# First stage of a graph network kernel: four counted superblocks ahead of the gathered ones, the other eleven between them, and the stage's buffers laid out anew

## The reference

```python
# gated layer
src_h = h[src] @ W_msg.T + b_msg
msg = src_h + edge_embed[clip(edge_type, 0, 8)]
messages = segment_sum(msg, dst, num_segments=N)
x = layernorm(x + gru_cell(messages, x))
# three layers, edges turned round, with a self loop on every node
h = concat(x[dst], edge_attr @ enc)      # the first one adds them
agg = segment_sum(h, src)
x' = relu(batchnorm(agg @ w1 + b1)) @ w2 + b2
# result: layernorm(x + layers(x))
```

## Time and profile before

| | us |
|---|---|
| median of three runs | 5869.93 |
| profiled execution | 5869.73 |
| its span | 5868.0 |
| PE busy | 5116.0 (87%) |
| DVE busy | 3763.8 (64%) |
| ACT busy | 3325.4 (57%) |
| POOL busy | 4223.4 (72%) |

### The profile page before, as it was taken

The page is one execution under the profiler, slowest core; times in us unless marked ns, Lnnn a source line. Parts: engine busy times, 40 slices in busy tenths (PEclk is TensorE's granted clock), DMA queues, the critical chain, the costliest instruction groups (busy, mean ns, idle before and its releaser), DMA issues.

```text
span 5868.0 us, 88444 instructions
## 1 busy us (share of the span) xinstructions
PE 5116.0 (87%) x26429; PEld 3281.9 (56%) x26429; DVE 3763.8 (64%) x14165; ACT 3325.4 (57%) x4432; POOL 4223.4 (72%) x4243
## 2 busy tenths in 40 slices
PE   4498888888888387777779999998999998999998
PEld 1144444444444144444447777776777776777776
DVE  8699999999999376666744444443444443444444
ACT  1177777777777222222347677665666665666665
POOL 6777777777777777777157777776777776777775
PEclk9999999999999677877679999999999999999999
DMA  8287778788878444444256666667767777666765
GB/s 282 62 182 188 176 180 185 182 191 200 186 180 194 98 117 123 118 122 121 68 193 201 198 212 210 211 212 219 207 200 213 213 212 235 205 196 206 206 204 163
DMA packets 1068180, 1066.43 MB, mean 182 GB/s; under 512 B 494051, under 2 KB 784501, under 8 KB 1067701
## 3 DMA queue, kind: packets, MB, share of 16 engines
q1 hardware_dynamic: 889573, 782.05, 47.6%
q0 software_dynamic: 178128, 278.65, 17.9%
HBM read 747.21 MB, written 216.68 MB: 164 GB/s over the span
## 4 chain that ended last, share of the span: by engine, by line
PE 44%; POOL 10%; issue 4%; DMA 3%; DVE 2%; ACT 1%; SPq 1%; DVEq 0%; ACTq 0%
PE ps L2965 27%; POOL GL L3051 7%; PE ps L2935 5%; POOL BIG L3033 3%; PE ps L2848 2%; PE ps L2809 2%; PE ps L2899 2%; PE ps L2810 2%; DVE BIG L2197 1%; PE ps L2909 1%; PE ps L2910 1%; DMA MS<-counts 1%; PE ps L2811 1%; DMA h_dense<-PCL 1%; PE ps L2914 0%
## 5 line engine op out<-in xcount | busy, mean ns | idle before, releaser
L3051 POOL DMA_INDIRECT GL<-h_gathered,IDXA x2058 | 2122.4, 1031 | 899.7 <-issue 615.4
L2965 PE MATMUL ps<-MSR,HP 128*128 128x512 f32 (+1 forms) x9000 | 2292.0, 402 | 56.0 <-ACT MSR L2575 36.6
L2575 ACT CAST MSR<-MS 128x1024 fp32r<-128x1024 uint8 (+1 forms) x1500 | 1509.3, 1029 | 959.0 <-PE ps L2965 867.5
L2965 PEld LDWEIGHTS ps<-MSR,HP 128*128 128x128 f32 x9000 | 1644.5, 190 | 449.4 <-ACT MSR L2575 57.9
L3017 POOL DMA_INDIRECT rec_q<-BIG x1563 | 1514.0, 969 | 521.6 <-issue 443.4
L2258 DVE CAST MSR<-MS 128x1024 fp32r<-128x1024 uint8 (+1 forms) x750 | 524.5, 700 | 1049.0 <-PE ps L2965 951.4
L2750 PE MATMUL ps<-MTB,XPS 128*128 128x512 bf16 x4410 | 1195.2, 387 | 1.0 <-DMA XPS<-x_parts 0.8
L2461 ACT CAST MTB<-MT 128x1024 bf16<-128x1024 uint8 x735 | 768.1, 1045 | 57.9 <-PE ps L2750 14.5
L3033 POOL DMA_INDIRECT BIG<-x_parts,SRCq x611 | 582.2, 953 | 188.1 <-issue 180.7
L2457 ACT CAST MT<-ps 128x512 uint16<-128x512 f32 x735 | 427.4, 582 | 343.6 <-PE ps L2733 328.9
L2750 PEld LDWEIGHTS ps<-MTB,XPS 128*128 128x128 bf16 x4410 | 414.7, 98 | 216.3 <-issue 20.0
(11 more groups left out here) (248 smaller groups left out, 5970.8 us busy)
## 6 DMA issues: line engine op xcount, KB each, us to landing
MS<-counts SPq DMA_DIRECT2D x1080, 256.0 KB, 3.4
counts<-BIG SPq DMA_DIRECT2D x360, 256.0 KB
XPS<-x_parts SPq DMA_DIRECT2D x192, 384.0 KB
GL<-h_gathered,IDXA POOLq DMA_INDIRECT x2058
rec_q<-BIG POOLq DMA_INDIRECT x1563
rec_q<-BIG SPq DMA_DIRECT2D x44, 490.0 KB, 10.9
HTI<-h_cols SPq DMA_DIRECT2D x72, 256.0 KB
h_dense<-PCL SPq DMA_DIRECT2D x30, 512.0 KB, 8.0
```

Of the source, the lines that this page charges most:

```text
L2575: s.copy(MSR[:, g % RM, :, 0:w].rearrange("p t (c s) -> p t c s", s=P), MSB[:, i % MR, 0:4 * w].rearrange("p (c h s t) -> p h t c s", h=2, ...
L2965: got = t.matmul(bank[:, 0:w], HP[:, d, part, :], MSR[:, g % RM, d % 2, 0:w], start=d + part == 0, stop=lay > 0 and d + part == BD, skip_g ...
L3051: g.indirect_dma_start(out=GL[:, r % LR, i, 0:3 * P], out_offset=None, in_=HGd[lay], in_offset=bass.IndirectOffsetOnAxis(ap=IDXA[:, a + i: ...
```

## The change

`node_groups()` now gives 0, 1, 2, 3, 15, 4, 16, 5, 17, 6, 18, 7, 19, 8, 9, 20, 10, 21, 11, 22, 12, 23, 13, 14, 24. DVE and SP wait at the stage's start for the counts stored and the records made (SP also for the last tiles placed); the wait for the scatters stands at slot PRELUDE = 66, the first gathered one (on DVE at that slot's one-hots). SP's index loads start there, and their chunks are spread over the slots behind it. POOL's own wait for the scatters stays; its gathers lose the wait that kept them near PE for the first 16 groups. `XG` and `SX` move behind the other buffers in BIG2. There are 409 slots in place of 408.

```diff
 def node_groups():
-    by_counts, gathered = list(range(JX)), list(range(JX, SG))
-    got = [by_counts.pop(0)]
-    while by_counts or gathered:
-        got += by_counts[:1] + gathered[:1]
-        by_counts, gathered = by_counts[1:], gathered[1:]
+    got, by_counts = list(range(4)), list(range(4, JX))
+    gathered = list(range(JX, SG))
+    for k, u in enumerate(gathered):
+        got.append(u)
+        n = len(gathered) - 1
+        got += by_counts[len(by_counts) * k // n:len(by_counts) * (k + 1) // n]
     return got
...
-INDEX_AT = [range(NS // IX * k // len(SLOTS), NS // IX * (k + 1) // len(SLOTS)) for k in range(len(SLOTS))]
+PRELUDE = GATHERED[QS0]
+
+def index_at(k):
+    if k < PRELUDE:
+        return range(0)
+    a, n = k - PRELUDE, len(SLOTS) - PRELUDE
+    return range(NS // IX * a // n, NS // IX * (a + 1) // n)
...
 def summed_beside(r):
-    return max(2 * r - 2, GATHERED[QS0 + r - QR] + 1 if r >= QR else 0)
+    return GATHERED[QS0 + r - QR] + 1 if r >= QR else 0
...
         ring = carve(BIG2)
-        XG = ring(QR * GT * XW // 2)...
-        SX = ring(QR * GT * 128)...
         SXD = ring(DR * GT * 128)...
...
         XB = ring(512)...
+        XG = ring(QR * GT * XW // 2)...
+        SX = ring(QR * GT * 128)...
...
# slot_onehots, gathered slot:
                 r = q - QS0
+                if r == 0:
+                    for i in range(3):
+                        for part in range(2):
+                            v.wait_ge(scat[i][part].sem, scattered(24 - (24 - i) % 3, part))
...
# first_vector:
-            for i in range(3):
-                for part in range(2):
-                    v.wait_ge(scat[i][part].sem, scattered(24 - (24 - i) % 3, part))
+            v.wait_ge(rec_made.sem, 3 + 3 * len(WIN))
...
# first_sync:
-            for i in range(3):
-                for part in range(2):
-                    y.wait_ge(scat[i][part].sem, scattered(24 - (24 - i) % 3, part))
+            y.wait_ge(placed.sem, len(PIECES))
+            y.wait_ge(rec_made.sem, 3 + 3 * len(WIN))
...
-            for i in range(2):
-                index_sync(y, i)
             for k, (_, _, steps) in enumerate(SLOTS):
+                if k == PRELUDE:
+                    for i in range(3):
+                        for part in range(2):
+                            y.wait_ge(scat[i][part].sem, scattered(24 - (24 - i) % 3, part))
+                    for i in range(2):
+                        index_sync(y, i)
```

More of the change, by code:

```diff
@@ L372 @@
 SLOTS = first_schedule()
-INDEX_AT = [range(NS // IX * k // len(SLOTS), NS // IX * (k + 1) // len(SLOTS)) for k in range(len(SLOTS))]
 COUNTED = {s[0]: i for i, s in enumerate(SLOTS) if s[1]}
 GATHERED = {s[0]: i for i, s in enumerate(SLOTS) if s[1] is False}
+PRELUDE = GATHERED[QS0]
[4 more added lines that the diff above has]
+    return range(NS // IX * a // n, NS // IX * (a + 1) // n)
+INDEX_AT = [index_at(k) for k in range(len(SLOTS))]
 def summed_beside(r):
-    return max(2 * r - 2, GATHERED[QS0 + r - QR] + 1 if r >= QR else 0)
+    return GATHERED[QS0 + r - QR] + 1 if r >= QR else 0
 def rows_summed(n):
@@ L1705, in program @@
         ring = carve(BIG2)
-        XG = ring(QR * GT * XW // 2).bitcast(BF16).rearrange("p (q i w) -> p q i w", q=QR, i=GT)
-        SX = ring(QR * GT * 128).bitcast(BF16).rearrange("p (q i w) -> p q i w", q=QR, i=GT)
         SXD = ring(DR * GT * 128).bitcast(BF16).rearrange("p (q i w) -> p q i w", q=DR, i=GT)
@@ L1714, in program @@
         XB = ring(512).rearrange("p (a c) -> p a c", a=4)
+        XG = ring(QR * GT * XW // 2).bitcast(BF16).rearrange("p (q i w) -> p q i w", q=QR, i=GT)
+        SX = ring(QR * GT * 128).bitcast(BF16).rearrange("p (q i w) -> p q i w", q=QR, i=GT)
         layers = ExitStack()
```

## The result

The changed kernel takes 5774.61 us (median of four runs, 5772.37 to 5782.62), the kernel before beside it 5866.66. The ratio is 0.9837, 95% interval 0.9825 to 0.9849 (the quotient of the two medians is 0.9843): faster by 1.6%, or 92 us by the medians. The forecast was 5773, in a range of 5757 to 5806.

The account below looks back on a forecast made before the run. Between two holes POOL's gathers set the stage's pace, PE and DVE working 157 us after them; 13, 14, 24 and the drain sum to 92.5 behind 23's end, so the layers start 96.6 earlier: 5869.7 - 96.6 = 5773, range 5757 to 5806.

Parts of the forecast that it names:

- 20, free of POOL: Gathered superblock 20 behind the doubled gap, without waits for POOL's gathers: 37.4 us in place of 47.6.
- a free pair: A counted and a gathered superblock, PE not waiting for POOL: 33.6 + 37.4 = 71.0 us, against 80.3 POOL-bound.
- layer start: The layers' first gather, at the stage's end: at 2886.8, 96.6 us earlier than before.
- The hole and the prelude: At the stage's start, during the scatters: nothing holds DVE or PE; four counted superblocks take 123.1 us from 1967.7.
- The ring: POOL's buffer of 16 groups: needed back at 2123.7, returned by PE at 2093, 30 us of room, no stop.
- the rival on the slower side: At 2123.7 POOL stands because the prelude is late, shifting all gathers; at 257 us for it 5877; chance 0.04.
- The doubled gap: Counted 8 and 9 before 20: 20 ends 21.4 us later, then 12.1, 2.8, then POOL-bound again by 23.
- the rival of slow gathered superblocks: Gathered superblocks run no faster free of POOL; after the doubled gap 23 ends 30.6 us late: 5804; chance 0.12.
- all hidden: The two counted superblocks before 24 are hidden too: 65 us more gained, 5708; chance 0.03.
- Scatters beside one-hots: Scatters beside the prelude keep pace; rival: collision moves gathers by up to 18 us, 5791, chance 0.07.
- The drain: From the last matmuls to the layers' first gather: 18 us taken, range 15.0 to 24, against 15.0 before.
- The layers: After the stage, work and loads are unchanged, so the 96.6 us gained reach the end whole.

Follow-up runs that it names:

- waits_only: Changed kernel with its later waits and buffers but the old order of superblocks: 5870.31 us, ratio 1.0005 to the kernel before.
- order_only: Changed kernel with its new order and buffers, but DVE and SP wait for the scatters at the stage's start as before: 5821.85 us, ratio 0.9920.
- front_six: Changed kernel with six counted superblocks in front, then gaps of 1, 1, 2, 1, 1, 2, 1, 0, 0 counted ones: 5754.12 us, ratio 0.9808.
- three_last: Changed kernel without the double gap before 20 and with three counted superblocks before 24: 5811.49 us, ratio 0.9900.
- none_behind: Changed kernel with the two counted superblocks before 24 moved into earlier gaps (2, 1, 1, 2, 1, 1, 2, 1, 0): 5723.60 us, ratio 0.9747.
- front_five: Changed kernel with five counted superblocks in front, then gaps of 2, 1, 1, 2, 1, 1, 1, 1, 0: 5731.31 us, ratio 0.9766.
- finish_later: none_behind with the six finishing steps of superblock 23 (dev to low) two slots later: 5724.13 us, ratio 0.9761.

## Why the prediction was right, step by step

| step | predicted | measured |
|---|---|---|
| first counted sum | 1967.7 | 1969.2 |
| four in front | 123.1 | 124.9 |
| first gathered sum | 2090.8 | 2094.1 |
| POOL stops | none | none |
| 8 and 9 | 65.2 | 66.7 |
| 20, free of POOL | 37.4 | 33.4 |
| a free pair | 71.0 | 67.2 |
| 23 ends | 2794.3 | 2794.1 |
| 13, 14, 24 | 74.5 | 76.7 |
| drain (from the start of the last matmuls) | 18 | 25.3 |
| layer start | 2886.8 | 2896.1 |
| layers | 2884.6 | 2874.6 |

**The hole and the prelude.** DVE's 77.6 at the scatters is gone, and four superblocks fit as reckoned. That this alone is worth nothing, and what it saves when joined with the order, waits_only and order_only show.

**The ring.** "30 us of room" held, and its edge is where the prediction put it: order_only and front_six stop when the ring has been full at 80.4 us, and the loss is about one for one. This was the rival on the slower side; its price is shown, its condition did not arise.

**The doubled gap.** 20 ended 20.4 us later behind the first gather than before (526.8 against 506.4), predicted 21.4, and 23 was POOL-bound again: it ended at 2794.1, predicted 2794.3. The free pace was mis-sized on the safe side, 33.4 for 37.4: I took off only PE's waits for gathers, but free of them PE also had its clock granted at 1.00 instead of 0.90 (an estimate: 37.25 busy us at 0.90 make 33.5 at 1.00). So the rival of slow gathered superblocks is out. So is the rival "all hidden": 13 and 14 stood behind 23 for 34.1 and 32.9 us.

**Scatters beside one-hots.** The group of the scatters inside the prelude stands against the last line of the earlier trace rows:

```profile
L3030 POOL DMA_INDIRECT rec_q<-BIG x60 | 58.1, 968 | 18.3 <-issue 18.3
```

968 ns in place of 957, beside 180 one-hots, is 0.7 us over all 60; this rival would have cost up to 18. The distance is (58.1 + 18.3) / 60 = 1.27 us, right at the limit that the prediction gave as a sign of being wrong, against 1.26 before, so that limit was set too tight. The Trainium skill (SBUF — State Buffer, "Who interferes with whom") states that a tensor_scalar in a 2-port mode blocks GpSimd. The trace does not show a blocking for these one-hots; in which mode they ran, no row tells.

**The drain** is the term that I mis-sized: "I take 18, near the row", where the upper bound was 24 and 25.3 came. Counted from the end of the last matmul, as the 15.0 of before, it is 24.7. Before, one node was left behind the last matmul; now two are. The timeline of the changed kernel, from the first sum of node 96 over that of node 97 and the deviation of superblock 23 to the two last statistics and SP's last store:

```profile
2871.00 0.56 DVE L2147 TENSOR_REDUCE BIG<-ps 128x128 f32<-128x384 f32 x1 [5.64 <-PE ps L2861]
...
2874.11 0.54 DVE L2147 TENSOR_REDUCE BIG<-ps 128x128 f32<-128x384 f32 x1
...
2876.92 1.28 ACT L2546 ACT_TABLE_LOAD   x1
2878.21 0.30 ACT L2546 ACTIVATE BIG<-BIG,EP 128x4 f32<-128x4 f32 x1
2878.42 0.24 ACT L2533 COPY BIG<-ps 10x128 f32<-10x128 f32 x1
...
2886.96 0.18 DVE L2180 BATCH_NORM_AGGREGATE BIG<-BIG 128x2 f32<-128x6 f32 x1
...
2889.48 0.18 DVE L2180 BATCH_NORM_AGGREGATE BIG<-BIG 128x2 f32<-128x6 f32 x1
...
2893.23 0.47 SPq L3225 DMA_DIRECT2D h_cols<-XT  x1
```

Node 97 needs 15.4 us from its sum to its statistic, where the last node before needed 7.1. The upper bound counted a second chain of 7.1 behind the first; in fact the chains run interleaved with each other and with the finishing steps of 23, and these 8.2 us more have three parts. The gate matmuls begin 4.9 us after the sum in place of 1.6: 2.2 us of the difference PE is still at node 96's, and 1.0 ACT is at the table load and the deviation of 23. They take 4.9 us in place of 2.6, with the clock granted at 0.50 (the lower level, 1.2 GHz) in place of 1.00 (2.4 GHz); it had been 1.00 from 2871.0 to 2874.0, with PE busy for 1.97 of the 3.00 us, and 0.59 from there to 2876.9. The windows of these matmuls are first of the changed kernel, then of the one before:

```profile
2878.90:2883.90 5.00, 4.93 (x9) 2.64 (x10) 1.46 (x6) 1.30 (x2) 0.00 (x0) 0.50 0.17 52
```

```profile
2970.10:2972.70 2.60, 2.58 (x8) 1.35 (x8) 1.22 (x5) 0.00 (x0) 0.00 (x0) 1.00 0.00 0
```

And from their end to the statistic it is 5.6 us in place of 2.9, behind node 96's tanh and statistic. The sum itself begins 2.7 us behind the last matmul in place of 0.1, and from the statistic to the layers' first gather it is 6.6 in place of 7.8; that makes the 9.7 between 15.0 and 24.7. All seven kernels that end with 24 lie above 18, from the end of the last matmul: 24.7 here, 22.2 in order_only, 22.7 in three_last, 22.0 in none_behind, 24.3 in front_five, 21.9 in front_six and 22.1 in finish_later. The two long ones are those whose gate matmuls of node 97 ran at 0.50 throughout (4.9 us in both; 2.6 to 3.7 in the others).

**The layers.** I said that their part "reaches the end whole". In the two profiles the stage gained 87.3 us (2983.4 to 2896.1) and the layers another 10. I do not take that for an effect of the change: their code is the same in all nine kernels, and from the layers' first gather to the span's end they took 2884.6 before, 2874.6 after, 2875.2 in waits_only (whose stage ends as late as before's), 2876.6, 2884.4 in three_last, 2879.0, 2878.2, 2880.4 and 2878.4. It looks like scatter between executions, some 10 us wide: the profiled execution of waits_only was the shortest of its ten (5864.48, median 5870.31), that of three_last the longest of its four (5814.93, median 5811.49). No kernel was profiled twice, so this is argued and not shown. In the superblock of the layers where three_last lost 5 us to waits_only (40.9 and 35.9 us), more of the waits are for counts from DRAM, first three_last, then waits_only:

```profile
DVE MSR L2269 <- DMA MS<-counts: 10.3, 3, 6.1
ACT MSR L2586 <- DMA MS<-counts: 8.7, 3, 6.6
```

```profile
DVE MSR L2270 <- DMA MS<-counts: 7.3, 3, 2.8
ACT MSR L2587 <- DMA MS<-counts: 5.1, 3, 3.3
```

So the 5773 came out closer than its working deserves: the layer start was missed by 9 us (7 drain, 2 superblocks behind 23; the sort's end, 3 us later, was made good by 23), and a good execution of the layers gave as much back. By layer starts counted from the first gather the change is worth 90.4, predicted 96.6; by the medians 92.

## What to carry to other kernels

Where one engine's stream bounds a stage, look at what has to follow its last item: only what leaves that place shortens the stage, and idle time ahead of the stream is worth just as much as it lets leave there. Work for the other engines fits between the stream's items as long as the ring in between neither fills up (in front, or behind two blocks in a row) nor the last item finds them late; free pace and ring depth, both readable from windows, and the drain of the changed kernel gave the time of the best order tried, none_behind, to within 2 us before it ran (5722 and 5723.6; in the profile its drain came out 2.3 shorter and the sort ended 2.3 later, which cancelled). When the last pieces come closer together, count the drain again with their chains one behind the other.

## What the runs showed of the hardware that was not expected

PE's granted clock went with what PE had to do: gathered superblocks whose gathers had landed ran at 0.97 to 1.00, 33 to 34 us each, counted ones with many small matmuls and waits at 0.55 to 0.70, 32 to 36 us each, in the hole (0.55 to 0.65) as later. The time of a counted one hardly followed its clock: 33.6 us at 0.64 and 33.7 at 0.70 before, 33.8 at 0.58 after. And the same layer code took from 2874.6 to 2884.6 us in nine profiles, a width of 10 us, where the runs of one kernel lie 7 to 22 us apart.
